# A gated-attention and mixture-of-experts block: first normalisation moved to GpSimd, loads and top-k bookkeeping moved in their queues

## What is computed

```python
x = x + tanh(g_xattn) * attention(layernorm(x), ctx, ctx)   # 32 query heads on 8 kv heads, D = 16
h = layernorm(x)
probs = softmax(h @ Wr)                  # 32 experts, the 4 best of each token
shared = silu(h @ Wsg) * (h @ Wsu) @ Wsd * sigmoid(h @ Wse)
routed = sum over a token's 4 experts: w * (silu(h @ Wg[e]) * (h @ Wu[e])) @ Wd[e]   # at most 64 tokens an expert
out = x + tanh(g_ffn) * (shared + routed)
```

## Time and profile before

| what | value |
|---|---|
| median of 3 runs | 2386.41 (2386.19 to 2386.46) |
| the profiled execution's own time | 2388.18 |
| its span | 2386.1 |
| first stage | 0 to about 795 |
| second stage | about 795 to 2386.1 |
| busy over the span | PE 96%, DVE 50%, ACT 32%, POOL 25% |

### The profile page before, as it was taken

How to read it: one execution, slowest core, us unless ns; L and a number is a source line. 1 busy time by engine, 2 the same in 40 slices (tenths; PEclk the granted TensorE clock), 3 DMA queues, 4 the chain that set the end, 5 groups by cost and what they waited for, 6 DMA issues and landing times.

```text
span 2386.1 us, 40464 instructions
## 1 busy us (share of the span) xinstructions
PE 2298.2 (96%) x12289; PEld 1755.6 (74%) x12289; DVE 1183.4 (50%) x2348; ACT 771.3 (32%) x1184; POOL 604.2 (25%) x1395
## 2 busy tenths in 40 slices
PE   7999999999999899999999999999999999999999
PEld 5666666666666687777777777777787777877777
DVE  6888888989898772223323233232232223322232
ACT  5777777777777210101101011010110101101010
POOL 5666666666665210000000000000000000000100
PEclk9999999999999899999999999999999999999999
DMA  3445544444545322321232212222222222322321
GB/s 82 130 130 130 131 128 131 128 131 128 131 129 142 111 40 94 130 78 62 90 106 81 77 63 93 101 81 77 66 97 95 81 77 66 110 81 86 123 81 42
DMA packets 276363, 235.09 MB, mean 99 GB/s; under 512 B 129505, under 2 KB 203233, under 8 KB 276322
## 3 DMA queue, kind: packets, MB, share of 16 engines
q1 hardware_dynamic: 271970, 221.89, 31.2%
q0 software_dynamic: 4352, 12.65, 1.9%
HBM read 161.88 MB, written 71.57 MB: 98 GB/s over the span
## 4 chain that ended last, share of the span: by engine, by line
PE 65%; DVE 1%; DMA 0%; issue 0%; DVEq 0%; POOLq 0%
PE acc L1118 7%; PE p_u L1134 7%; PE p_u L1136 7%; PE p_u L1135 7%; PE acc L1119 7%; PE acc L1120 7%; PE p_g L1134 7%; PE p_g L1136 7%; PE p_g L1135 7%; PE p_x L1166 2%; PE p_y L1153 2%; PE p_x L1153 2%; PE p_x L1144 0%; PE p_y L1159 0%; DMA rows<-out_dram 0%
## 5 line engine op out<-in xcount | busy, mean ns | idle before, releaser
L1052 DVE TENSOR_TENSOR act_f<-p_u,act_f 128x512 f32<-128x512 f32 x176 | 121.7, 692 | 984.5 <-PE p_u L1136 984.3
L957 ACT ACTIVATE act_f<-p_g 128x512 f32<-128x512 f32 x176 | 105.2, 598 | 1215.5 <-PE p_g L1136 1194.9
L555 DVE TENSOR_REDUCE negmax<-p_max 128x8 fp32r<-128x1024 f32 x256 | 311.9, 1218 | 74.4 <-PE p_max L703 74.4
L437 ACT ACTIVATE probs<-p_exp 128x1024 f32<-128x1024 f32 x256 | 262.0, 1023 | 99.0 <-PE p_exp L662 98.8
L1118 PE MATMUL acc<-wd_h,hh 128*128 128x512 f32 x704 | 279.5, 397 | 0.0
L1134 PE MATMUL p_u<-xh,wgu_h 128*128 128x512 f32 x704 | 274.1, 389 | 3.6 <-DVE act_f L1052 3.6
L1134 PE MATMUL p_g<-xh,wgu_h 128*128 128x512 f32 x704 | 275.5, 391 | 0.0
L1119 PE MATMUL acc<-wd_l,hh 128*128 128x512 f32 x704 | 274.3, 390 | 0.0
L1120 PE MATMUL acc<-wd_h,hl 128*128 128x512 f32 x704 | 274.3, 390 | 0.0
L1136 PE MATMUL p_g<-xh,wgu_l 128*128 128x512 f32 x704 | 274.0, 389 | 0.0
L1136 PE MATMUL p_u<-xh,wgu_l 128*128 128x512 f32 x704 | 274.0, 389 | 0.0
(11 more groups left out here) (142 smaller groups left out, 3492.1 us busy)
## 6 DMA issues: line engine op xcount, KB each, us to landing
ew<-in_L_ffn_Wg_dram SPq DMA_DIRECT2D x32, 704.0 KB
ew<-in_L_ffn_Wu_dram SPq DMA_DIRECT2D x32, 704.0 KB
xs<-in_x_dram SPq DMA_DIRECT2D x64, 256.0 KB, 3.6
xres<-in_x_dram SPq DMA_DIRECT2D x64, 256.0 KB, 2.9
out_dram<-x SPq DMA_DIRECT2D x64, 256.0 KB, 2.1
xn_rows<-xn SPq DMA_DIRECT2D x64, 256.0 KB, 3.1
xn_cols<-xnT SPq DMA_DIRECT2D x64, 256.0 KB, 2.9
rows<-out_dram SPq DMA_DIRECT2D x16, 1024.0 KB, 5.3
```

The source lines that it names most:

```text
L437: nc.scalar.activation(probs[c][:, :], p_exp[:, :, :].rearrange("p a b -> p (a b)"), ACT.Exp, scale=float(D) ** -0.5).then_inc(exp_done, 1)
L555: nc.vector.tensor_reduce(negmax[c // 2][:, 0:16].rearrange("p (g c i) -> p c i g", g=2, c=2)[:, c % 2, :, :].bitcast(F32R), p_max[:, :, : ...
```

## The change

- `norm_x` moves from VectorE to GpSimd. It stands behind the inverse root for the same batch (B+2), so it also runs one turn earlier than before.
- GpSimd's top-four bookkeeping becomes `take_top`. It handles B-5 instead of B-4 and stands behind `q_stacks`, ahead of the inverse roots; one call more stands behind the loop. The tiles it reads (lg, v8, idx_f, is_top) get two buffers each, and VectorE's copy of the logits waits for the bookkeeping of two batches back instead of one.
- SyncE's `load_in(B + 3)` moves from c = 1 to c = 2, behind the four DMAs of the maxima.
- `stats_x` gets a wait for VectorE's own last aggregation (stat1).
- `FIRST` is 7 instead of 5.

```diff
-            FIRST, LAST = 5, 61
+            FIRST, LAST = 7, 61
@@ SyncE
                         if c == 1:
-                            if (B + 3).ok:
-                                load_in(B + 3)
                             if B.ok:
                                 wait(sp, pv_mm, 2 * (B.n - 1))
...
+                        if c == 2 and (B + 3).ok:
+                            load_in(B + 3)
                         if c == 2 and (B - 2).ok:
                             b = B - 2
                             wait(sp, x2_done, b.n + 1)
@@ GpSimd
+                def norm_x(b):
+
+                    pool.wait_ge(rs1_done, b.n + 1)
+                    wait(pool, qs_done, b.n - 1)
+                    alone(pool, spare_p)
+                    nc.gpsimd.tensor_scalar(qraw[b.par][:, :], xs[b.par][:, :], mv1[b.par][:, 0:1], rs1[:, 0:1],
+                                            ALU.subtract, ALU.mult).then_inc(qraw_done, 1)
...
+                def take_top(b):
+
+                    pool.wait_ge(top_done, b.n + 1)
...
                 def body(B):
...
                     if (B + 1).ok:
                         k_stacks(B + 1)
                         q_stacks(B + 1)
+                    if (B - 5).ok:
+                        take_top(B - 5)
                     if (B + 2).ok:
                         inverse_root(B + 2, stat1, mv1, ve1, rs1, qraw_done, rs1_done)
+                        norm_x(B + 2)
                     if (B - 2).ok:
                         inverse_root(B - 2, stat2, mv2, ve2, rs2, xn_done, rs2_done)
...
-                    b = B - 4
-                    if b.ok:
-
-                        pool.wait_ge(top_done, b.n + 1)
...
                 iterations(pool, body, chain)
+                take_top(Batch((NB - 2) // 2, 1))
@@ VectorE
                 def stats_x(b):
                     dve.wait_ge(x_in[b.par], 16 * (b.half + 1))
+                    wait(dve, stat1, b.n)
                     return stats(xs[b.par][:, :], st1)
...
-                def norm_x(b):
-                    wait(dve, qs_done, b.n - 1)
-                    layer_norm(b, xs, mv1, rs1, rs1_done, qraw, qraw_done)
...
-                            wait(dve, kept, b.n)
-                            nc.vector.tensor_copy(lg[:, :], p_ot[:, 0:NE + 1]).then_inc(lg_done, 1)
+                            wait(dve, kept, b.n - 1)
+                            nc.vector.tensor_copy(lg[b.par][:, :], p_ot[:, 0:NE + 1]).then_inc(lg_done, 1)
...
-                        if c == 0:
-                            if (B + 1).ok:
-                                norm_x(B + 1)
-                            if (B + 2).ok:
-                                x_stats = stats_x(B + 2)
+                        if c == 0 and (B + 2).ok:
+                            x_stats = stats_x(B + 2)
```

More of the change, by code:

```diff
@@ L163, in build @@
             mhalf = sb("mhalf", [128, 1])
-            lg = sb("lg", [128, NE + 1])
-            v8 = sb("v8", [128, 8])
+            lg = [sb(f"lg{i}", [128, NE + 1]) for i in range(2)]
+            v8 = [sb(f"v8_{i}", [128, 8]) for i in range(2)]
             i8 = sb("i8", [128, 8], U32)
             iota_e = sb("iota_e", [128, NE])
-            idx_f = sb("idx_f", [128, TOPK])
-            is_top = sb("is_top", [128, TOPK, NE])
+            idx_f = [sb(f"idx_f{i}", [128, TOPK]) for i in range(2)]
+            is_top = [sb(f"is_top{i}", [128, TOPK, NE]) for i in range(2)]
             two_sum = sb("two_sum", [128, 2, NE])
@@ L364, in q_stacks @@
                     last.then_inc(qs_done, 1)
+                def take_top(b):
+                    pool.wait_ge(top_done, b.n + 1)
+                    alone(pool, spare_p)
+                    nc.gpsimd.tensor_copy(top_val[:, bass.ts(b.n, TOPK)], v8[b.par][:, 0:TOPK])
+                    nc.gpsimd.tensor_copy(gate_z[:, bass.ts(b.n, 1)], lg[b.par][:, NE:NE + 1])
+                    nc.gpsimd.tensor_copy(top_idx[:, bass.ts(b.n, TOPK)], idx_f[b.par][:, :])
+                    nc.gpsimd.tensor_tensor(two_sum[:, :, :], is_top[b.par][:, 0:2, :], is_top[b.par][:, 2:4, :], ALU.add).then_inc(kept, 1)
+                    pool.wait_ge(kept, b.n + 1)
+                    alone(pool, spare_p)
+                    chain.inc(nc.gpsimd.tensor_tensor(one_sum[:, :], two_sum[:, 0, :], two_sum[:, 1, :], ALU.add))
+                    chain.wait(pool)
+                    alone(pool, spare_p)
+                    nc.gpsimd.tensor_tensor(chosen[:, bass.ts(b.n, 1), :].rearrange("p a e -> p (a e)"), one_sum[:, :],
+                                            key_of[:, bass.ts(b.n, 1)].to_broadcast([128, NE]), ALU.mult)
                 def body(B):
@@ L382, in body @@
                         nc.gpsimd.tensor_tensor(w_cols(wgu_l, B.pair), wst_cols, w_cols(wgu_h, B.pair).bitcast(F32), ALU.subtract).then_inc(wlo_done, 1)
-                    b = B - 4
-                    if b.ok:
-                        pool.wait_ge(top_done, b.n + 1)
[L387 to L392, removed]
-                        pool.wait_ge(kept, b.n + 1)
-                        alone(pool, spare_p)
-                        chain.inc(nc.gpsimd.tensor_tensor(one_sum[:, :], two_sum[:, 0, :], two_sum[:, 1, :], ALU.add))
-                        chain.wait(pool)
-                        alone(pool, spare_p)
-                        nc.gpsimd.tensor_tensor(chosen[:, bass.ts(b.n, 1), :].rearrange("p a e -> p (a e)"), one_sum[:, :],
-                                                key_of[:, bass.ts(b.n, 1)].to_broadcast([128, NE]), ALU.mult)
                 chain.per_turn = 2 * (1 + 1 + 1 + 1 + 1)
                 iterations(pool, body, chain)
+                take_top(Batch((NB - 2) // 2, 1))
             @block.scalar
@@ L571, in body @@
                             alone(dve, spare_d)
-                            chain.inc(nc.vector.max(v8[:, :], lg[:, 0:NE]))
+                            chain.inc(nc.vector.max(v8[B.par][:, :], lg[B.par][:, 0:NE]))
                             top_count = chain.value()
@@ L583, in body @@
                             alone(dve, spare_d)
-                            chain.inc(nc.vector.tensor_copy(idx_f[:, :], i8[:, 0:TOPK]))
+                            chain.inc(nc.vector.tensor_copy(idx_f[B.par][:, :], i8[:, 0:TOPK]))
                             top_count = chain.value()
```

9 lines of the change are left out of this document (5 added, 4 removed).

## The result

| kernel | median | runs | profiled run's own time | its span |
|---|---|---|---|---|
| before | 2386.3 | 4 | 2388.18 | 2386.1 |
| after | 2348.99 (2347.16 to 2351.92) | 4 | 2348.52 | 2346.6 |

The ratio after to before is 0.9846, with a 95% interval of 0.9829 to 0.9863. The kernel is 37 us faster; 51 were forecast, and the time lies inside the range of 2315 to 2364. It lies 1 above the band of the forecast's own case (2322 to 2348), and nearer to rival B's 2357 than to 2335. The direction held, and so did the account of what was late in the kernel before. What bounds the kernel after is rival B's mechanism, and most of what follows is about why.

The account below looks back on a forecast made before the run. In the first stage neither TensorE nor VectorE was a clean bound; waits between them mattered. Iterations 48.4, loop entry 2.4, start -0.9 and end 1.1 gave 51 off 2386.1, so 2335, range 2315 to 2364.

Parts of the forecast that it names:

- rival B: GpSimd becomes the bound and xn waits for its root: 22.8 an iteration, 2357; chance 0.18.
- loop entry and the first turns: At loop entry TensorE waited for late maxima, then ran at a lower clock; 2.4 comes back without that.
- late chain: Bookkeeping waits for VectorE, delaying key and query splits, SyncE's kv load and maxima; TensorE's waits of 0.48 and 0.77 go.
- The price of GpSimd's norm: The normalisation on GpSimd takes 0.9 (0.6 to 1.37), 1.0 with its wait, and hides behind TensorE and VectorE.
- The split turn, 11.1: VectorE is late for its next maximum, so the norm's 0.45 all lies on the path: 11.57 becomes 11.1.
- The load turn, 10.9: VectorE's own work falls from 10.73 to 10.3; new collisions add 0.6, making 10.9.
- Collisions, 0.6 in the load turn: VectorE's cast, xn, is_top and x2 may now wait for GpSimd instructions: 0 to 1.2, taken as 0.6.
- The start: GpSimd does keys after the normalisation instead of beside it: -0.9 (-1.5 to 0).
- The end: VectorE's wait of 1.11 for the bookkeeping at the end goes: +1.1 (0 to 1.1).
- rival C: The moved loads delay the second set of maxima by 1.5, a turn takes 12.1, slower at 2401; chance 0.05.
- Rival A: VectorE's collisions mostly miss and TensorE's floor sets both turns: 21.2 an iteration, 2313; chance 0.12.
- D: No change: removed waits are replaced one for one, as the xnT store holds SyncE instead: 2386; chance 0.05.

Follow-up runs that it names:

- e1: The kernel before with only the loads of x and kv moved to c = 2 behind the maxima: 2363.73.
- e2: The kernel before with only GpSimd's bookkeeping moved behind the query splits, with its second buffers and FIRST = 7: 2369.69.
- e3: The kernel after with the first normalisation put back on VectorE, so only loads and bookkeeping are moved: 2367.22.
- e5: The kernel after with two constants in GpSimd's norm instruction, leaving out the normalisation of the queries: 2332.39.
- e9: The kernel after with one per-partition operand and a constant in GpSimd's norm, leaving out the subtraction of the mean: 2331.81.
- e11: e8 with every second norm, the one from GpSimd's turn with the weight piece, put back on VectorE: 2368.82.
- e8: The kernel after with the 1 MB load for the second stage issued at the end of turn 64 instead of turn 61: 2345.3.
- e12: e10 with GpSimd's turn put in the order in which its inputs come, the weight piece moved to the next turn: 2326.34.
- e10: e8 with the first norm as a ScalarE activation, and GpSimd's root for B+2 ahead of the query splits: 2394.91.

## Why the prediction was right, and where it was off

**By terms.** The forecast's sum against what the two profiled executions show (span 2386.1 and 2346.6, so 39.5):

| term | forecast | measured | how read |
|---|---|---|---|
| iterations | +48.4 (28 x 1.73) | +38.9 (28 x 1.39) | 23.73 - 22.34 |
| loop entry and the first turns | +2.4 | +3.8 | the rest, up to x2 at 701.25 |
| start | -0.9 | -1.9 | first maximum at 19.76, before at 17.87 |
| end | +1.1 | -1.2 | from that x2 to the last product: 54.76, before 53.56 |

**The bottleneck and the late chain: right.** The one chain that the forecast named (bookkeeping waits, key and query splits late, SyncE held at kv, maxima late) was the cause of both of TensorE's waits. e1 and e2 show it from both sides: each of two quite different edits removes the wait for the maxima, and e2 the one for the query splits too. What the forecast did not see is that they are two cures for one illness. It let the wait of 0.77 go by the loads' move; e3 against e2 shows that beside the moved bookkeeping this move brings nothing that can be measured.

**The price of GpSimd's norm: wrong, and it decides.** This is the step that failed. It took 0.9, from one-input instructions with constants, with 1.37 as the high end; it is 2.09, beyond the end. By the forecast's own working, with 2.2 in place of 1.0 for the norm and its wait, GpSimd comes to 18.6 + 2 x 2.2 = 23.0 an iteration, above the 22.0 of the other engines; it gave 22.34, because GpSimd's other instructions shrank from 15.8 to 86.86 x 22.34 / 100 - 2 x 2.09 = 15.2, with 2.9 of gaps. So rival B came true in its mechanism (GpSimd as the bound, xn waiting for its root), at a milder size than its 22.8. e5 and e9 show that this one price is the difference: with 0.62 or 0.70, near what the forecast assumed, the kernel takes 2332, within 3 of the forecast. The range held because B's case was inside it, not because its own case came true: that is luck in part. The cover was called thin, and the doubt should have gone into the high end: the rows it rested on had no operand that differed by partition, and a form that no row shows can cost more than any row.

The Trainium skill, GPSIMD Engine Reference, section "When to use GPSIMD", says that with one input GpSimd runs at roughly line rate. The measurement agrees for constants, 0.62 against VectorE's 0.54, and disagrees for this form of one input tile and two operands that differ by partition, 2.09, which is 3.9 times VectorE's time with the same two.

**The split turn, 11.1: nearly right** (11.16 to 11.20), but by other causes than the forecast's, which had the cast's 0.5 in it. The cast is free, and xn is stretched by 0.43 in its place. That the whole 0.45 of the norm lies on the path was not shown either: behind it in the same turn the kernel before has a wait of 0.38 for TensorE's scores, at 568.27. **The load turn, 10.9: wrong**, it is 11.17 as well. In both turns TensorE waits 0.37 to 0.38 for xn (574.33 and 585.49), in the load turn through the late root, in the split turn through the piece.

**Collisions, 0.6 in the load turn: wrong in place and in size.** In that turn only is_top is stretched, by about 0.1. In the split turn xn loses 0.43 and is_top 0.1, the cast wins 0.5 back and x2 0.29. From 100 to 700 the averages went from 0.93 to 0.75 for x2, 0.43 to 0.19 for the cast, 0.54 to 0.76 for xn and 0.28 to 0.37 for is_top: a little less in sum than before, where more was forecast. The forecast looked for what GpSimd's new work would meet and not for what its old work would no longer meet.

The Trainium skill, SBUF — State Buffer, section "SBUF: two separate sides", has an exclusive lock here, held for a whole instruction; it names as VectorE's side of it instructions in a 2-port mode or with two SBUF inputs, a condition that the forecast left out. The rows agree with such a lock, but a part of the held instruction gets by. In the kernel after xn began 0.26 behind wgu_l and ended 0.30 after it (585.24 against 584.94); in e11 it began 0.57 behind it (578.45, shown at e11) and ended 0.28 after it:

```profile
579.02 0.65 DVE L513 TENSOR_SCALAR xn<-x,mv,rs 128x512 f32<-128x512 f32 x1
```

It ended about 0.3 after the piece whether it began early or late, as an instruction would that is held until the piece is done and has some 0.25 of its 0.55 behind it by then. While GpSimd's 2.09 ran, VectorE's maxima, which read PSUM, took their usual times (1.23 and 1.23 at 579.91 and 582.08).

**The start.** -0.9 had taken the price of 0.9 as well. The norm now runs 2.10 (9.58 to 11.68) ahead of the key splits, which before ran beside VectorE's: 1.9 late. It is the same mis-sized price again.

**The end.** The 1.11 was counted as a gain and the turns at the end as unchanged. The 1 MB load had already been seen in the earlier trace rows, with a wait of 1.42 behind it. In the kernel after it stands directly ahead of the maxima and the wait is 2.07. The forecast priced this collision for the moved loads (rival C) and forgot it for the load that was there. e8 gives the size: from the same x2 to the last product it takes 753.04 - 702.20 = 50.84 in place of 54.76, so the end is 2.7 faster than before there and not 1.2 slower. The kernel as a whole gains 3.7 in the medians.

**Rival C, the moved loads delay the maxima: no.** TensorE's waits for maxima are 4.0 in all, at the ends. **Rival A and D: no.** A's floor of 21.2 was too low by 0.4 to 0.5: TensorE, all but without waits, makes 21.6 in the shortest iterations of e5 and 21.7 in e12.

## What to carry to other kernels

An instruction that moves to another engine has to be priced in its exact form there, with its operands; the price of a similar form may be off by three times, and where the engine's cover is thin that price decides everything. In a queue executed in order, each instruction should stand behind those whose inputs come before its own; a wait ahead of ready work cost 24 us in the kernel before (e1), and another was among the causes of the 69 between e10 and e12. An instruction that moves also changes what runs beside what: look for the collisions that go as well as for those that come. A busy share below 100 is no room by itself: GpSimd was busy 75 of 100 in e11 and yet late. Count the work between two waits.

## What the runs showed of the hardware that was not expected

- GpSimd's tensor_scalar on 128x512 float32: 0.62 with two constants, 0.70 with one per-partition operand, 2.09 with two (subtract, then multiply). VectorE takes 0.54 and ScalarE 0.81 (as scale and bias of an activation) for the same normalisation. (Whether the pair of operands or the pair of operations makes the last form slow is open.)
- A 1 MB load issued 0.5 ahead of four small DMAs made the last of these land 3.5 after its issue (708.63 to 712.09), against 1.1 where no load stood ahead.
- One pause of TensorE of 2.07 was followed by a stretch with a granted clock of 0.55, and the turn cost more than the pause's own length: the step took 14.51 against 10.63 without it, 3.9, and the stage ended 3.0 later.
- VectorE's tensor_scalar of 0.55 that began 0.26 or 0.57 behind a GpSimd instruction of 0.94 ended 0.30 or 0.28 after that one's end, and x2 took 0.75 in the kernel after and 1.10 to 1.17 beside the query splits in e2; the maxima over PSUM took 1.23 beside GpSimd's 2.09.
